# New places for the side operations of a four-layer kernel, and the order in which its waits are written

## The chip, the cores and the metric

The kernel runs on one core of one Trainium2 chip. The metric is the device time of one execution in microseconds (us); the median of several executions is given. A core has five engines that matter here, each with its own in-order stream of instructions: PE (TensorE, matrix products), DVE (VectorE), ACT (ScalarE), POOL (GpSimd) and SP, which here only issues DMAs. They meet through semaphores: an instruction that ends raises one, another instruction waits for its value.

## The reference

Thirty-two sequences of 256 rows and 256 channels pass four layers one after the other. Two of them are selective state-space layers, which are computed as a recurrence over the 256 rows; one is softmax attention with 16 heads, one is linear attention. Cut to what sets the work:

```python
def step(hst, inp):                      # layers 0 and 2, 512 channels x 16 states
    dt_t, B_t, C_t, x_t = inp
    dA = jnp.exp(dt_t[:, :, None] * A)
    hst = hst * dA + (dt_t * x_t)[:, :, None] * B_t[:, None, :]
    return (hst, jnp.einsum('bds,bs->bd', hst, C_t))

att = jnp.einsum('bnhl,bmhl->bnmh', q, k)            # layer 1
att = jax.nn.softmax(att + (1.0 - mask) * -1000000.0, axis=2)
y = jnp.einsum('bnmh,bmhl->bnhl', att, v)

attn = jnp.einsum('bhse,bhsd->bhed', softmax(k), v)  # layer 3, linear in the rows
y = jnp.einsum('bhtd,bhed->bhte', softmax(q), attn)

x = L0(x); x = L1(x); x = L2(x); x = L3(x)           # each adds its result to x
```

Every layer begins with a layer norm and is modulated by a condition vector.

## The kernel before

Two sequences form a group (512 columns side by side); there are 16 groups. The backbone of the program is the recurrence. For one layer and one group it takes 32 **steps**, each over 128 channels and two states at once (a tile of 128 x 1024). Step s consists of:

- `exp{s}` on ACT (L975): the decay factors into one of three tiles `da`;
- `dbx{s}` on DVE (L1025): the input term into the PSUM tile `z`, of which there is one;
- `scan{s}` on DVE (L1039): the recurrence along the rows, out of `da` and `z` into one of four tiles `hw`;
- `mul{s}` and `add{s}` on POOL (L1057, L1064): times C, and the two states added;
- `red{s}` on PE (L926): a product with the identity that sums in PSUM.

The four `hw` tiles are a ring: `scan{s}` waits for `red{s-4}`. `dbx{s}` waits for `scan{s-1}`, since it overwrites `z`, and `scan{s}` waits for `dbx{s}`. So DVE alternates between two operations that each wait for the one ahead of them on the same engine. SP loads the slices `bs` and `cs` of B and C for every step, broadcast to all partitions.

Everything else is a **side operation**. It is written as pieces: `front` (layer norm, input projection, convolution), `mid` and `rest` (step sizes: `d` on PE, then `ab`, `e`, `l` on ACT, `dt` on DVE, `dtx` on POOL; gates `z`), `back` (output projection, residual), `attn_a`/`attn_b` (softmax attention, one sequence each) and `lin_a`/`lin_b` (linear attention). In **one round** of the loop 64 steps are done: 32 of the first recurrence (segment 0) with the pieces attn_b, front1, rest0, back1, lin_a and mid1 beside them, and 32 of the second (segment 1) with back0, attn_a, front0, rest1, lin_b and mid0. The groups are pipelined across rounds: each segment works on other groups than the pieces beside it.

What sets the order is the table `PLACES`. For each piece and each engine it has one number for each part of that piece. A part with the number 27.73 is written on its engine behind what the recurrence puts at lower numbers: whole numbers are `dbx` on DVE, s + 0.33 is `scan` (the table `AT`), s + 0.3 is a reduction on PE, s + 0.1 an `exp` on ACT, s + 0.05 and s + 0.55 are `mul` and `add` of step s - 1 on POOL. So a DVE number between s and s + 0.33 puts an operation between `dbx` and `scan`, one between s + 0.33 and s + 1 puts it between `scan` and the next `dbx`. There is no scheduler at run time; every engine works its list off in this order and stands when the operation at its head isn't ready.

In attention, eight pairs of heads each take four score products on PE (L1277) into two of three PSUM banks; DVE takes the row maxima out of them (`mx{p}0`, `mx{p}1`, L1397), and a bank is free for a later pair when its maximum is taken. Later the products are formed again the other way round (L1304), exponentiated on ACT (L1372) and multiplied with the values (L1320).

## Time and profile before

| | |
|---|---|
| median of 3 runs | 5507.8 us (5505.3 to 5511.87) |
| the profiled execution, its own time | 5501.84 us |
| span from first to last instruction of it | 5500.1 us |
| granted TensorE clock, mean | 0.885 of full |
| busy: PE / DVE / ACT / POOL | 4551.2 / 4640.8 / 3256.8 / 4061.4 us |

The span begins with a prologue that loads weights and makes constants, then the pipeline of groups fills; from about 0.5 ms to 4.9 ms it is in its steady state, in which every round does the same work in the same order; at the end it drains. The busy share of an engine is an average over all this, so the questions of what waits for what are asked of the steady state.

### The profile page before, as it was taken

How to read it: one execution, taken by the hardware profiler on the slowest of the kernel's cores; microseconds unless marked ns; L12 is line 12 of the kernel's file. 1: busy time of each engine (PE TensorE's matmuls, PEld its weight loads, DVE VectorE, ACT ScalarE, POOL GpSimd, SP SyncE). 2: the span in 40 equal slices, each digit the busy share in tenths (PEclk: the TensorE clock that was granted, in tenths of full speed). 3: DMA queues.
4: the chain of work that ended last, by engine and by line, in shares of the span. 5: the costliest groups of instructions: out<-in, count | busy, mean ns of one | idle time of the engine just before them, and what ended most of it. 6: DMA issues, size and time to landing. Idle time of an engine off the chain costs nothing.

```text
span 5500.1 us, 54997 instructions
## 1 busy us (share of the span) xinstructions
PE 4551.2 (83%) x16792; PEld 2433.0 (44%) x16792; DVE 4640.8 (84%) x4711; ACT 3256.8 (59%) x5572; POOL 4061.4 (74%) x2838
## 2 busy tenths in 40 slices
PE   4577888988889888888888888888988888888755
PEld 1243444444444444444454444444444444444423
DVE  2729899998999899999989999999989889999373
ACT  2335566666666666666666666666666666666252
POOL 1718787887878787887878788787878778787172
PEclk8668899999999899999999999999999899998775
DMA  4616666766766666676667667676667667666161
GB/s 147 215 46 230 221 233 223 238 231 221 245 216 233 223 235 225 223 248 216 234 217 237 220 230 237 219 246 210 236 221 240 219 221 248 219 230 219 37 208 53
DMA packets 355068, 1164.54 MB, mean 212 GB/s; under 512 B 39355, under 2 KB 79348, under 8 KB 354774
## 3 DMA queue, kind: packets, MB, share of 16 engines
q1 hardware_dynamic: 310614, 1106.42, 59.6%
q10 hardware_dynamic: 44160, 54.60, 3.1%
q8 instruction: 135, 2.21, 0.2%
q14 instruction: 159, 1.30, 0.1%
HBM read 1140.78 MB, written 20.10 MB: 211 GB/s over the span
## 4 chain that ended last, share of the span: by engine, by line
PE 41%; DVE 28%; issue 10%; POOL 9%; ACT 8%; DMA 3%; SPq 1%; DVEq 0%; ACTq 0%; POOLq 0%
DVE hw L1039 15%; PE ps L926 7%; DVE ps L1025 7%; PE ps L698 5%; PE ps L1231 5%; PE ps L1277 4%; POOL hw L1057 4%; PE ps L1304 3%; PE ps L1222 3%; PE ps L1320 2%; DVE mx L1397 2%; PE ps L707 2%; ACT da L975 2%; POOL hw L1064 2%; PE ps L669 1%
## 5 line engine op out<-in xcount | busy, mean ns | idle before, releaser
L1057 POOL TENSOR_TENSOR hw<-hw,cs 128x1024 f32<-128x1024 f32 x1024 | 2413.2, 2357 | 698.7 <-DVE hw L1039 636.2
L1039 DVE TENSOR_TENSOR_SCAN hw<-da,ps 128x1024 f32<-128x1024 f32 x1024 | 2335.4, 2281 | 94.9 <-ACT da L975 21.2
L975 ACT ACTIVATE da<-dt,a_neg 128x510 f32<-128x510 f32 x2048 | 1332.1, 711 | 193.7 <-DVE hw L1039 191.2
L1064 POOL TENSOR_TENSOR hw<-hw 128x512 f32<-128x512 f32 x1024 | 1297.9, 1267 | 66.3
L926 PE MATMUL ps<-hw,ident 128*128 128x512 f32 x2048 | 1184.0, 683 | 180.7 <-POOL hw L1064 180.6
L1025 DVE TENSOR_TENSOR ps<-ps,bs 128x1024 f32<-128x1024 f32 x1024 | 1256.6, 1227 | 67.0 <-DMA bs<-bc_scratch 7.1
L926 PEld LDWEIGHTS ps<-hw,ident 128*128 128x128 f32 x2048 | 399.9, 213 | 634.0 <-issue 322.6
L698 PE MATMUL ps<-hT,w_in 128*128 128x512 f32 x1024 | 534.5, 658 | 68.7 <-DVE dt L886 47.8
L1372 ACT ACTIVATE pts<-ps 128x512 f32<-128x512 f32 x512 | 278.5, 593 | 441.7 <-PE ps L1304 441.7
L1397 DVE TENSOR_REDUCE mx<-ps 128x2 f32<-128x512 f32 x512 | 332.0, 681 | 166.5 <-PE ps L1277 165.6
L1277 PE MATMUL ps<-k,q 32*128 32x256 f32 x2048 | 354.3, 469 | 112.5 <-DVE mx L1397 112.0
L570 ACT ACT_TABLE_LOAD x319 | 409.3, 1283 | 5.6
L698 PEld LDWEIGHTS ps<-hT,w_in 128*128 128x128 f32 x1024 | 200.5, 206 | 344.8 <-issue 209.8
L1277 PEld LDWEIGHTS ps<-k,q 32*128 32x128 f32 x2048 | 217.1, 219 | 300.8 <-DVE mx L1397 183.3
L1304 PE MATMUL ps<-q,k 32*128 32x256 f32 x2048 | 301.6, 412 | 21.0 <-ACT pts L1372 21.0
L1320 PE MATMUL ps<-pts,va 128*32 128x256 f32 x2048 | 269.8, 397 | 2.8 <-ACT pts L1372 2.6
L909 POOL TENSOR_TENSOR dtx<-dt,u 128x512 f32<-128x512 f32 x128 | 162.2, 1268 | 142.8 <-DVE dt L886 142.4
L1304 PEld LDWEIGHTS ps<-q,k 32*128 32x128 f32 x2048 | 185.1, 191 | 144.7 <-ACT pts L1372 63.3
L1139 PE MATMUL ps<-w_out,dtx 128*128 128x256 f32 x1024 | 240.3, 389 | 3.4 <-DVE dtx L1008 1.8
L713 PE MATMUL ps<-xd,w_dt 97*128 97x512 f32 x256 | 170.4, 753 | 80.3 <-POOL dtx L909 54.5
L707 PE MATMUL ps<-u,taps 128*128 128x512 f32 (+3 forms) x512 | 229.0, 590 | 0.0
L1139 PEld LDWEIGHTS ps<-w_out,dtx 128*128 128x128 f32 x1024 | 195.8, 194 | 57.7 <-issue 30.8
(178 smaller groups left out, 5306.8 us busy)
## 6 DMA issues: line engine op xcount, KB each, us to landing
bs<-bc_scratch SPq DMA_DIRECT2D x1024, 512.0 KB, 4.4
cs<-bc_scratch SPq DMA_DIRECT2D x1024, 512.0 KB, 4.9
taps<-taps_scratch SPq DMA_DIRECT2D x32, 512.0 KB, 5.5
xhat<-in_x ACTq DMA_DIRECT2D x16, 512.0 KB, 7.2
gate<-gates_scratch ACTq DMA_DIRECT2D x64, 128.0 KB, 5.2
x_b<-in_x ACTq DMA_DIRECT2D x16, 512.0 KB, 7.6
x_scratch<-x_b ACTq DMA_DIRECT2D x16, 512.0 KB, 3.4
x_c<-x_scratch ACTq DMA_DIRECT2D x16, 512.0 KB, 6.4
```

What stands on the lines that cost most here:

```text
L570: nc.scalar.preload_act_table_set(name)
L698: ins = nc.tensor.matmul(side[pc.bank[f"m{m}"]], w_in[l][:, k, m * P:(m + 1) * P], hT[:, k, :], start=(k == 0), stop=(k == DC - 1))
L926: nc.tensor.matmul(yps, ident[:, :], hw[q % RING][:, 0, :], start=False, stop=(q % PER == PER - 1))\
L975: ins = nc.scalar.activation(da[q % (AHEAD + 1)][:, k, :, 1:S], dt_[:, c, :].rearrange("p (b s) -> p b s", b=GB)[:, :, 1:S], ACT.Exp, scal ...
L1025: nc.vector.tensor_tensor(z, dxp.unsqueeze(1).broadcast_to([P, 2, T]), bs[s % B_RING][:, :, :], ALU.mult)\
L1039: nc.vector.tensor_tensor_scan(tile[:, :, :].rearrange("p n t -> p (n t)"), da[s % (AHEAD + 1)][:, :, :, :].rearrange("p n b s -> p (n b s)"),
L1057: nc.gpsimd.tensor_tensor(tile[:, :, :], tile[:, :, :], cs[s % C_RING][:, :, :], ALU.mult)\
L1064: nc.gpsimd.tensor_tensor(tile[:, 0, :], tile[:, 0, :], tile[:, 1, :], ALU.add)\
L1139: ins = nc.tensor.matmul(side[pc.bank[key]][:, k * D:(k + 1) * D], dtx[l][:, c, r * P:(r + 1) * P], w_out[l][:, c, :], start=(c == 0), sto ...
L1277: ins = nc.tensor.matmul(banks[hh][:, t * S:(t + 1) * S], q4[rr, h // 4, t * P:(t + 1) * P], k4[rr, h // 4, :], start=True, stop=True)
L1304: ins = nc.tensor.matmul(banks[hh][:, t * S:(t + 1) * S], k4[rr, h // 4, t * P:(t + 1) * P], q4[rr, h // 4, :], start=True, stop=True)
L1397: nc.vector.tensor_reduce(mx[:, :, h // 4, at0], side[pc.bank[f"s{p}{hh}"]].rearrange("p (t s) -> p t s", t=RB), X, ALU.max, negate=True). ...
```

## The change

All tables in `PLACES` get new numbers: nearly every side operation on PE, ACT, DVE and POOL stands a little earlier or later among the steps. No operation is added or removed. On ACT the number of loads of function tables stays at 321. Besides, the order in which waits are written is turned in five spots: in `scan_vector` for `dbx` and for `scan`, in `times_c` for `mul`, and in `attn_tensor` for both kinds of score products.

```diff
     "mid1": {
-        "pe": [29.55, 29.675, 29.8, 29.925, 30.05, 30.175],
+        "pe": [28.586, 28.729, 28.871, 29.014, 29.157, 30.8],
...
@@ scan_vector
-                if s % PER == 0:
-                    dve.wait_ge(pc.of(f"dxp{c}"), pc.upto(g, f"dxp{c}"))
-                dve.wait_ge(*b_slice(l, g, s))
                 if s:
                     dve.wait_ge(pc.of(f"scan{s - 1}"), pc.upto(g, f"scan{s - 1}"))
...
+                if s % PER == 0:
+                    dve.wait_ge(pc.of(f"dxp{c}"), pc.upto(g, f"dxp{c}"))
+                dve.wait_ge(*b_slice(l, g, s))
                 nc.vector.tensor_tensor(z, dxp.unsqueeze(1).broadcast_to([P, 2, T]), bs[s % B_RING][:, :, :], ALU.mult)\
...
                 yield s + AT["scan"]
+                dve.wait_ge(pc.of(f"dbx{s}"), pc.upto(g, f"dbx{s}"))
                 dve.wait_ge(pc.of(f"exp{s}"), pc.upto(g, f"exp{s}"))
...
-                dve.wait_ge(pc.of(f"dbx{s}"), pc.upto(g, f"dbx{s}"))
@@ times_c
+            pool.wait_ge(pc.of(f"scan{s}"), pc.upto(g, f"scan{s}"))
             pool.wait_ge(*c_slice(l, g, s))
-            pool.wait_ge(pc.of(f"scan{s}"), pc.upto(g, f"scan{s}"))
@@ attn_tensor (both score products)
-                for hh in range(2):
+                for hh in (1, 0):
```

```order
L1025 TENSOR_TENSOR ps<-ps,bs 128x1024 [waits scan1_dve,b_slice1_1_in]
L1039 SCALAR_TENSOR_TENSOR hw<-da,ps 128x1024 [waits scan1_dve,scan1_pe,scan1_act]
L1177 TENSOR_TENSOR ps<-ps,gate 128x512 [waits front1_pool,gate0_in,front1_dve,back0_pe,front1_act,front1_pe]
L1185 TENSOR_TENSOR x_b<-x_b,ps 128x512 [waits back0_dve,residual_in]
L1177 TENSOR_TENSOR ps<-ps,gate 128x512 [waits back0_pe]
L1185 TENSOR_TENSOR x_b<-x_b,ps 128x512 [waits back0_dve]
L623 BN_STATS stats<-x_b 128x6 [waits back0_dve,back0_act,back0_pe]
```

And in the changed program:

```order
L1039 SCALAR_TENSOR_TENSOR hw<-da,ps 128x1024 [waits scan1_pe,scan1_act,scan1_dve]
L1177 TENSOR_TENSOR ps<-ps,gate 128x512 [waits front1_pool,gate0_in,front1_dve,back0_pe,front1_act,front1_pe]
L1185 TENSOR_TENSOR x_b<-x_b,ps 128x512 [waits back0_dve,residual_in]
L1177 TENSOR_TENSOR ps<-ps,gate 128x512 [waits back0_pe]
L1185 TENSOR_TENSOR x_b<-x_b,ps 128x512 [waits back0_dve]
L1025 TENSOR_TENSOR ps<-ps,bs 128x1024 [waits b_slice1_0_in,scan1_dve]
L623 BN_STATS stats<-x_b 128x6 [waits back0_dve,back0_act,back0_pe]
```

The wait of `dbx` and `scan` for DVE's own preceding operation (`scan1_dve`) has moved from the semaphore instruction onto the operation; the side operations keep their waits.

The second is DVE in segment 1, steps 11 to 13, where the maxima of `attn_a` are taken. Before:

```order
L1039 SCALAR_TENSOR_TENSOR hw<-da,ps 128x1024
L1397 TENSOR_REDUCE mx<-ps 128x2 x3
L886 SCALAR_TENSOR_TENSOR dt<-ps,dt 128x512
L1397 TENSOR_REDUCE mx<-ps 128x2
L1025 TENSOR_TENSOR ps<-ps,bs 128x1024
L1397 TENSOR_REDUCE mx<-ps 128x2 x2
L623 BN_STATS stats_b<-x_c 128x6 x2
L1397 TENSOR_REDUCE mx<-ps 128x2 x2
L628 COPY small<-one_col 128x1
L630 BN_AGGR mv_b<-stats_b 128x2 x2
L1039 SCALAR_TENSOR_TENSOR hw<-da,ps 128x1024
L1397 TENSOR_REDUCE mx<-ps 128x2 x3
```

And now:

```order
L1039 SCALAR_TENSOR_TENSOR hw<-da,ps 128x1024
L1397 TENSOR_REDUCE mx<-ps 128x2 x4
L1025 TENSOR_TENSOR ps<-ps,bs 128x1024
L1397 TENSOR_REDUCE mx<-ps 128x2 x3
L623 BN_STATS stats_b<-x_c 128x6 x2
L1397 TENSOR_REDUCE mx<-ps 128x2
L628 COPY small<-one_col 128x1
L630 BN_AGGR mv_b<-stats_b 128x2 x2
L1397 TENSOR_REDUCE mx<-ps 128x2 x5
L1039 SCALAR_TENSOR_TENSOR hw<-da,ps 128x1024
L1397 TENSOR_REDUCE mx<-ps 128x2 x2
```

Between `dbx12` and `scan12` there are nine maxima in place of four.

The third is PE at the end of segment 0, from the output product of `lin_a` (L1222, `out`) over the projection of `mid1` (L722, four products) and its step size `d0` (L713) to `rest1` (L713, L698); L926 are the reductions. Before:

```order
L926 MATMUL ps<-hw,ident 128x512
L1214 MATMUL ps<-rows,ones 128x512
L1222 MATMUL ps<-w_l_out,hT_b 128x256 x4
L926 MATMUL ps<-hw,ident 128x512
L722 MATMUL ps<-u,w_xp 96x512 x4
L713 MATMUL ps<-xd,w_dt 128x512
L926 MATMUL ps<-hw,ident 128x512 x2
L713 MATMUL ps<-xd,w_dt 128x512
L698 MATMUL ps<-hT,w_in 128x512 x4
```

And now:

```order
L926 MATMUL ps<-hw,ident 128x512
L1214 MATMUL ps<-rows,ones 128x512
L1222 MATMUL ps<-w_l_out,hT_b 128x256 x4
L926 MATMUL ps<-hw,ident 128x512
L722 MATMUL ps<-u,w_xp 96x512 x4
L713 MATMUL ps<-xd,w_dt 128x512
L926 MATMUL ps<-hw,ident 128x512 x3
L713 MATMUL ps<-xd,w_dt 128x512
L698 MATMUL ps<-hT,w_in 128x512 x2
```

The neighbours are the same, but the whole chain from `out` to `d0` stands one reduction earlier: the reduction between `out` and the projection was that of step 27 and is now that of step 26.

## Rows read from the trace of the kernel before

**Rows 1.** The page, part 1: busy us (share of span), number of instructions.
```profile
PE 4551.2 (83%) x16792; PEld 2433.0 (44%) x16792; DVE 4640.8 (84%) x4711; ACT 3256.8 (59%) x5572; POOL 4061.4 (74%) x2838
```
**Rows 2.** Windows: window, us; busy of PE, PEld, DVE, ACT, POOL; clock, DMA, GB/s.
```profile
883.48:4342.05 3458.57, 3014.19 (x11507) 1628.67 (x11506) 3169.03 (x3190) 2231.48 (x3829) 2787.95 (x1937) 0.92 0.68 229
```
**Rows 3.** Waits of DVE, 883 to 4342 us: us in total, times, longest.
```profile
DVE mx L1397 <- PE ps L1277: 77.3, 65, 3.1
DVE dt L886 <- ACT dt L823: 34.3, 24, 1.8
DVE dtx L1008 <- PE ps L926: 18.1, 29, 1.6
DVE stats L623 <- DMA xhat<-in_x: 17.5, 11, 2.3
DVE small L1564 <- ACT kT L1503: 15.3, 11, 2.6
DVE hw L1039 <- ACT da L975: 14.5, 32, 0.7
```
**Rows 4.** Timeline of DVE, bare steps, then side operations (start, us, engine, line).
```profile
2126.28 2.29 DVE L1039 TENSOR_TENSOR_SCAN hw<-da,ps 128x1024 f32<-128x1024 f32 x1
2128.67 1.23 DVE L1025 TENSOR_TENSOR ps<-ps,bs 128x1024 f32<-128x1024 f32 x1
2130.03 2.29 DVE L1039 TENSOR_TENSOR_SCAN hw<-da,ps 128x1024 f32<-128x1024 f32 x1
...
2133.79 2.29 DVE L1039 TENSOR_TENSOR_SCAN hw<-da,ps 128x1024 f32<-128x1024 f32 x1
2135.99 0.68 DVE L1177 TENSOR_TENSOR ps<-ps,gate 128x512 f32<-128x512 f32 x1
2136.77 0.69 DVE L1185 TENSOR_TENSOR x_b<-x_b,ps 128x512 f32<-128x512 f32 x1
2137.38 0.69 DVE L1177 TENSOR_TENSOR ps<-ps,gate 128x512 f32<-128x512 f32 x1
2138.10 0.69 DVE L1185 TENSOR_TENSOR x_b<-x_b,ps 128x512 f32<-128x512 f32 x1
```
**Rows 5.** Timeline of POOL in a stretch without side operations.
```profile
2110.88 1.27 POOL L1064 TENSOR_TENSOR hw<-hw 128x512 f32<-128x512 f32 x1
...
2114.53 1.27 POOL L1064 TENSOR_TENSOR hw<-hw 128x512 f32<-128x512 f32 x1
```
**Rows 6.** Timeline of PE in the scores of attn_a: two pairs of heads.
```profile
2166.74 1.31 PE L1277 MATMUL ps<-k,q 32*128 32x256 f32 x8 [1.48 <-DVE mx L1397]
2168.86 2.08 PE L1277 MATMUL ps<-k,q 32*128 32x256 f32 x8 [0.81 <-DVE mx L1397]
```
**Rows 7.** Timeline, end of segment 0, from `cv3_3` to `dt1`.
```profile
2097.12 1.02 PE L926 MATMUL ps<-hw,ident 128*128 128x512 f32 x2
2098.92 3.65 PE L722 MATMUL ps<-u,w_xp 128*96 128x512 f32 x8 [0.78 <-issue]
2106.46 0.69 DVE L886 SCALAR_TENSOR_TENSOR dt<-ps,dt 128x512 f32<-128x512 f32 x1 [1.80 <-ACT dt L823]
2112.05 0.69 DVE L886 SCALAR_TENSOR_TENSOR dt<-ps,dt 128x512 f32<-128x512 f32 x1 [1.34 <-ACT dt L823]
```
**Rows 8.** Timeline, load of the next group: `xo`, the DMA issue, first use.
```profile
2220.85 0.68 DVE L1421 TENSOR_TENSOR x_b<-ps,x_b 128x512 f32<-128x512 f32 x1
...
2221.70 0.39 ACTq L582 DMA_DIRECT2D xhat<-in_x  x1
...
2228.94 1.40 DVE L623 BATCH_NORM_STATS2 stats<-xhat 128x6 f32<-128x256 f32 x4 [1.46 <-DMA xhat<-in_x]
```
**Rows 9.** The page, part 5: the recurrence's groups with idle time before them.
```profile
L1057 POOL TENSOR_TENSOR hw<-hw,cs 128x1024 f32<-128x1024 f32 x1024 | 2413.2, 2357 | 698.7 <-DVE hw L1039 636.2
L1039 DVE TENSOR_TENSOR_SCAN hw<-da,ps 128x1024 f32<-128x1024 f32 x1024 | 2335.4, 2281 | 94.9 <-ACT da L975 21.2
L1025 DVE TENSOR_TENSOR ps<-ps,bs 128x1024 f32<-128x1024 f32 x1024 | 1256.6, 1227 | 67.0 <-DMA bs<-bc_scratch 7.1
```

More of the change, by code:

```diff
@@ L200 @@
     "mid0": {
-        "pe": [27.729, 27.871, 28.014, 28.157, 28.633, 28.967],
-        "act": [27.814, 28.5, 28.7, 28.9],
-        "dve": [31.11, 31.22],
-        "pool": [31.217, 31.383],
+        "pe": [27.9, 28, 28.1, 28.2, 28.633, 28.967],
+        "act": [28.433, 28.656, 28.767, 28.989],
+        "dve": [31.22, 31.83],
+        "pool": [31.217, 32.05],
         "sp": [30.533, 30.867],
@@ L214 @@
     "rest0": {
-        "pe": [0.633, 3.967, 4.5, 4.9, 5.967, 7.467, 8.133, 10.767],
-        "act": [-1.5, 2.3, 4.6, 4.767, 4.933, 7.8, 8.267, 8.767, 8.933],
-        "dve": [3.165, 9.165, 11.165, 13.165],
-        "pool": [3.3, 9.3, 11.3, 11.8],
+        "pe": [-1.333, 4.8, 5.7, 6.1, 6.9, 7.8, 9.78, 10.98],
+        "act": [1.767, 3.6, 5.6, 5.85, 7.7, 7.9, 8.35, 9.475, 9.6],
+        "dve": [4.165, 9.777, 10.665, 14.11],
+        "pool": [4.3, 10.3, 11.3, 15.217],
         "sp": [-0.909, -0.818],
@@ L242 @@
     "back0": {
-        "pe": [2.1, 3.467, 3.633, 3.8, 3.967],
-        "act": [1.767, 3.433, 3.767, 6.3],
-        "dve": [5.414, 5.498, 5.581, 5.665, 5.749],
-        "pool": [4.717, 4.883],
+        "pe": [3.443, 3.586, 3.729, 3.871, 4.014],
+        "act": [-1.75, 4.35, 4.85, 6.267],
+        "dve": [5.442, 5.553, 5.665, 5.777, 5.888],
+        "pool": [4.3, 4.425],
         "sp": [-0.545, -0.455],
@@ L249 @@
     "back1": {
-        "pe": [11.967, 14.05, 15.7],
-        "act": [10.6, 13.6],
-        "dve": [13.665, 14.165, 15.665, 16.11, 16.22],
-        "pool": [16.217, 16.383],
+        "pe": [11.9, 14.8, 18.767],
+        "act": [10.85, 17.35],
+        "dve": [14.22, 14.665, 16.665, 17.141, 17.189],
+        "pool": [15.383, 18.717],
         "sp": [-0.727, -0.636],
@@ L1294, in attn_tensor @@
                     banks = [side[pc.bank[f"t{p}{hh}"]] for hh in range(2)]
-                    for hh in range(2):
+                    for hh in (1, 0):
                         if p == 0 and hh == 0:
```

82 lines of the change are left out of this document (41 added, 41 removed), and 6 rows, old and new, of the table PLACES.

## The prediction, made before the changed kernel had run

> **What bounds the kernel now.** I read the page's busy times first: DVE is busy for 84% of the span, PE for 83%, POOL for 74% [rows 1]. A mean over filling and draining says little, so next the window that holds eleven whole rounds, from one start of `back0` to another: 3458.57 us, 314.4 us a round [rows 2]. There DVE is busy for 3169.03 us, 92%, PE for 87%, POOL for 81%, at a mean granted clock of 0.92. DVE is the engine that the round's length follows; what can be won is the time in which it stands, 289.5 us in the window or 26.3 us a round.
>
> That time is of two kinds. The waits list gives the long stands [rows 3]: maxima that wait for score products 77.3 us, step sizes that wait for ACT 34.3, the gated output that waits for a reduction 18.1, the statistics of the next group that wait for its DMA 17.5, the linear attention's reciprocal 15.3, scans that wait for their exponentials 14.5. These six make 177.0 us; with the smaller ones I estimate 19 us a round. The other kind no list names: in the timeline [rows 4] a scan begins at 2126.28 and lasts 2.29 us, `dbx` starts at 2128.67, 0.10 us behind it, and the next scan 0.13 us behind that one's end, though nothing but DVE's own preceding operation was awaited. The page's idle before scan and before `dbx`, 94.9 and 67.0 us in the whole run with small named parts [rows 9], is mostly this.
>
 An operation that waits for nothing fresh even starts before the one ahead has ended: the scan that began at 2133.79 ends at 2136.08, L1177 behind it starts at 2135.99, an overlap of 0.09 us. So a side operation in a gap hides the gap, and only gaps without one can win. Counted in DVE's order, before has 425 scans directly behind their `dbx` and 473 `dbx` directly behind a scan; the changed program has 468 and 547, because it bunches its side operations more. Before: 425 x 0.13 + 473 x 0.10 = 103 us. After: 1015 x 0.035 = 36 us. Against that, 117 more bare pairs lose an overlap of 0.09 us each, 10 us. Sum: -57 us. Part of it will be eaten, since DVE, arriving sooner, stands longer where PE, ACT or a DMA comes last; with a fifth off I take **-45 us**. Bounds: 0, if every time saved ends in another engine's wait, and -67 us.
>
> POOL limits this as well. Its shortest step, from one `add` to the next, is 2114.53 - 2110.88 = 3.65 us [rows 5]; DVE's bare step is now 3.75 us (2126.28 to 2130.03) and would be 3.59. Where many bare steps follow each other, POOL becomes the slower one and caps the gain at 0.10 instead of 0.16 a step. The ring of four lets DVE run ahead by some 3 steps and most bare stretches are short, so this is inside the fifth taken off. The turned waits of `mul` and of the score products I cost at nothing on the path where DVE is far ahead (POOL waits 636.2 us for scans [rows 9], it has room), and at 0.07 us for each pair of scores that DVE waits for: 0.07 x 16 pairs a round at most 1.1 us a round; I take none of it, it is in the lower bound.
>
> There is a page that speaks against this term. In the Trainium skill, VectorE: DVE Perf Modes, section "The DRAIN you can't avoid", eight copies with a semaphore after each are stated to take as long as eight with one at the end: a wait for one's own engine costs nothing. By that rule the sum would lack these 45 us. The two L1185 [rows 4] say otherwise, since the same dependence costs 0.10 or 0.03 us depending on where its wait sits.
>
> **The places, stand by stand.** Times of a stand are read per round and compared with the new order.
> - Maxima. The 77.3 us [rows 3] are 7.0 a round; by their places in the timeline 2.9 fall on `attn_b` in segment 0 and 4.1 on `attn_a` in segment 1. In `attn_b` the first moves from behind `scan4` to behind `dbx5` with `dt1` now ahead of it, 1.9 us later on DVE, the projections of keys and values that come before its products on PE stand one reduction earlier, and the input projection that stood between the first two pairs now follows the second. These stands should nearly go: -2.5.
> - In `attn_a` two pairs of products took 1.31 us near full clock and 2.08 us at half clock [rows 6]. With three banks, `mx{p}0` can't start sooner than one product time after `mx{p-1}0` ended, and between them DVE has one maximum of 0.7 us. Nine maxima now stand in one gap, with 1.1 us of statistics among them. At full clock four pairs leave about 4 x (1.3 - 0.6) - 1.1 = 1.7 us of idle, at half clock 4 x (2.2 - 0.6) - 1.1, less 1.2 us for a `dbx` within the first, = 4.1 us. PE works in bursts here, as it does now, and now it is at half clock here; I take 3.2 for the block: -0.9.
> - `dt0` of `mid1`, 1.80 us [rows 7]. The projection starts at 2098.92, behind a reduction that began at 2097.12. One reduction earlier in the list takes one of 1.02 us out from ahead of it, not a whole step, since `out` ahead of both keeps its time. 1.8 becomes 1.0: -0.8. `dt1` waits 1.34 us [rows 7] for a chain that starts at `dt0` (`dtx0`, `d1`, `ab1`, `e1`, `l1`, 5.6 us in all) over `dbx31` and `scan31`; order and chain stay, DVE gets there 0.2 us sooner: +0.2.
> - The reciprocal of the keys, 15.3 / 11 = 1.4 us [rows 3]. Its maximum moves half a step later and the chain of `front1` ahead of it on ACT gets a step more room: -1.2.
> - Scans that wait for `exp`, 1.3 us a round [rows 3], three spots. `exp2` of segment 1 now has one gate ahead of it instead of two, `exp11` of segment 0 no longer stands behind `l3`, `exp30` of segment 1 stands ahead of the convolution's end; but `exp31` then comes behind a whole `mid0` chain: -0.8.
> - The gated output, 18.1 / 11 = 1.6 us: its reductions get ahead of score products in two of three spots: -0.9.
> - The next group's load. `xo` begins at 2220.85, the DMA is issued at 2221.70 and its statistics begin at 2228.94 [rows 8], 7.4 us behind `xo`'s end. Between them now lie two scans and a `dbx` (5.9 us), then they will be two `dbx` and a scan (4.7 us): the stand grows from 1.5 to 2.7 us: +1.1.
>
> These make -2.5 - 0.9 - 0.8 + 0.2 - 1.2 - 0.8 - 0.9 + 1.1 = -5.8 us a round. A list of numbers written anew for four engines also makes stands that I haven't traced; half a microsecond at two or three spots is what before has in such small ones, so +1.3. That leaves -4.5 us a round, and 16 rounds (the last ones thin) make **-72 us**. Bounds: 0 (each stand comes back elsewhere) and -12 us a round, -190 us, if only `dt1`, the load and a few maxima are left of the 19.
>
> **Sum.** 5501.84 - 45 - 72 = 5385 us for an execution like the profiled one. The median shown is 6 us above it, 0.1%; I carry half of that over: **5388 us**, 2.2% below.
>
> **Rivals.**
> - The places bring nothing and only the waits do (each stand that goes is replaced). 5508 - 45 = 5463 us. For it: half of what the list names hangs on chains that keep their order, such as `dt1`. Against: three stands have a cause that the new order plainly removes.
> - The waits bring nothing, by the skill's rule or since POOL and PE take it back. 5508 - 72 = 5436 us.
> - The places bring more than I could trace, -10 us a round, and the waits all 57: 5508 - 217 = 5291 us.
> - Slower: TensorE takes the end. Its mean clock of 0.92 [rows 2] is a mix of full and half, so 16% of a round, 50 us, now run at half clock. A new list makes new gaps on PE, and where it stands the clock falls. Were the half-clock time doubled, 50 us of the round would do only 25 us of matmul work, at 87% busy 22 us more of PE time, against 40 us in which it stands now. A third of that, 7 us, reaching DVE would cancel the waits' and the places' gain together; half, 11 us, would give 5508 + 16 x (11 - 7.3) = 5567 us. It decides from about 35 us of additional half clock a round. Against it: score products, the one stretch where PE's stands are long, are stretches at half clock already.
> - Nothing measurable, 5508: gains cancelled by new stands.
>
> **How the numbers follow.** The forecast has a chance of 0.50 (5340 to 5440), places without effect 0.16, waits without effect 0.08, more than forecast 0.15, slower 0.07, no difference 0.04. A measurement of this kernel can tell about 0.2%, 11 us, from no change. So faster by over 0.2%: 0.89, within it 0.04, slower 0.07. The range leaves out the slower rival, no change and the far end of the best: 5300 to 5475.
>
> **What would show it.** Right: in the timeline 0.03 to 0.04 us between `dbx` and scan both ways, with the idle before L1039 and L1025 down from 162 us together to below 100, though bare pairs are more; waits of DVE for L1277 and L823 smaller, the one for the DMA of `xhat` larger, near 2.7 us a round. Wrong: gaps still at 0.10; a clock below 0.90 in the steady state; POOL's wait for scans near zero; or a DVE stand of several us in `attn_a` between `dbx12` and `scan12`.

## The result: slower, and the profile after

The changed kernel takes 5574.8 us (median of 4 runs, 5537.95 to 5590.66), the kernel before beside it 5507.4 us: ratio 1.0113, 95% interval 1.0074 to 1.0152. 5388 us had been forecast. The profiled execution, on which the rows below rest, took 5537.95 us and is the shortest of the four; what makes the others longer comes out below.

The page, part 1 (columns as in [rows 1]), and the window of eleven whole rounds (columns as in [rows 2]):

```profile
PE 4578.3 (83%) x16792; PEld 2422.8 (44%) x16792; DVE 4653.2 (84%) x4711; ACT 3259.9 (59%) x5572; POOL 4053.3 (73%) x2838
```
```profile
878.38:4373.63 3495.25, 3027.14 (x11508) 1619.32 (x11507) 3178.97 (x3190) 2234.75 (x3830) 2782.60 (x1937) 0.92 0.67 226
```

A round takes 3495.25 / 11 = 317.8 us instead of 314.4 [rows 2], at the same mean clock. DVE's work is nearly the same (3178.97 us busy for 3169.03 in the eleven rounds); what has grown is the time in which it stands.

**The short gaps are gone.** DVE's timeline of three bare steps (start, duration):

```profile
2115.97 2.29 DVE L1039 TENSOR_TENSOR_SCAN hw<-da,ps 128x1024 f32<-128x1024 f32 x1
2118.29 1.23 DVE L1025 TENSOR_TENSOR ps<-ps,bs 128x1024 f32<-128x1024 f32 x1
2119.56 2.29 DVE L1039 TENSOR_TENSOR_SCAN hw<-da,ps 128x1024 f32<-128x1024 f32 x1
```

The scan ends at 2118.26 and `dbx` starts at 2118.29; `dbx` ends at 2119.52, the next scan starts at 2119.56. In [rows 4] these gaps were 0.10 and 0.13 us. Over all bare pairs of the window the medians fall from 0.132 to 0.035 us ahead of a scan and from 0.104 to 0.035 us ahead of a `dbx`. All gaps of DVE under 0.3 us, overlaps counted as negative, sum to 32.5 us less, 3.0 us a round.

**The long stands have grown.** Those over 0.3 us rise from 208.1 to 278.5 us in the eleven rounds, by 6.4 us a round. The waits list of DVE, 880 to 4340 us (us in total, times, longest), to be held against [rows 3]:

```profile
DVE mx L1397 <- PE ps L1277: 100.2, 87, 2.5
DVE ps L1025 <- DMA bs<-bc_scratch: 46.1, 27, 3.7
DVE qsm L1557 <- PE ps L1222: 29.9, 11, 9.3
DVE dt L886 <- ACT dt L823: 22.6, 24, 1.4
DVE ps L1025 <- ACT ps L989: 17.6, 20, 2.0
DVE rec L1409 <- PE ps L1328: 17.2, 11, 1.6
```

The stands that the prediction wanted gone are smaller or not in the list: `dt` 22.6 us for 34.3, the gated output 1.1 for 18.1 and the next group's statistics 9.7 for 17.5 (both further down the list), the reciprocal of the keys gone from it. Three take their place: maxima 100.2 us for 77.3, `dbx` waiting for the B rows 46.1 us, and `qm`, the maximum over the queries of `lin_b` (L1557), 29.9 us. On the page the idle ahead of the scan falls and that ahead of `dbx` rises (to be held against [rows 9]):

```profile
L1039 DVE TENSOR_TENSOR_SCAN hw<-da,ps 128x1024 f32<-128x1024 f32 x1024 | 2333.6, 2279 | 37.0 <-ACT da L975 8.4
...
L1025 DVE TENSOR_TENSOR ps<-ps,bs 128x1024 f32<-128x1024 f32 x1024 | 1256.2, 1227 | 115.5 <-DMA bs<-bc_scratch 65.1
```

### The profile page after: what moved, and what is told of

The parts are those of the page before. It is cut to its first block, busy times and chain, and to the rows that moved or that the text cites. A ratio compares the mean times of both kernels' runs of the same rounds, so it can differ in the third digit from the quotient of the medians.

```text
span 5536.2 us, 54997 instructions
## 1 busy us (share of the span) xinstructions
PE 4578.3 (83%) x16792; PEld 2422.8 (44%) x16792; DVE 4653.2 (84%) x4711; ACT 3259.9 (59%) x5572; POOL 4053.3 (73%) x2838
## 4 chain that ended last, share of the span: by engine, by line
PE 48%; DVE 20%; ACT 10%; issue 8%; POOL 7%; DMA 5%; SPq 1%; ACTq 0%; DVEq 0%; POOLq 0%
PE ps L926 8%; DVE hw L1039 8%; PE ps L1231 5%; PE ps L1304 5%; PE ps L1277 4%; DVE ps L1025 4%; PE ps L1222 4%; POOL hw L1057 3%; PE ps L698 3%; ACT da L975 3%; PE ps L1139 3%; PE ps L707 3%; DVE mx L1397 3%; PE ps L1320 3%; DMA bs<-bc_scratch 2%
## 5 line engine op out<-in xcount | busy, mean ns | idle before, releaser
L1039 DVE TENSOR_TENSOR_SCAN hw<-da,ps 128x1024 f32<-128x1024 f32 x1024 | 2333.6, 2279 | 37.0 <-ACT da L975 8.4
L1025 DVE TENSOR_TENSOR ps<-ps,bs 128x1024 f32<-128x1024 f32 x1024 | 1256.2, 1227 | 115.5 <-DMA bs<-bc_scratch 65.1
L926 PE MATMUL ps<-hw,ident 128*128 128x512 f32 x2048 | 1178.4, 676 | 120.9 <-POOL hw L1064 120.6
L926 PEld LDWEIGHTS ps<-hw,ident 128*128 128x128 f32 x2048 | 397.4, 212 | 595.3 <-issue 326.9
L698 PE MATMUL ps<-hT,w_in 128*128 128x512 f32 x1024 | 525.3, 644 | 72.4 <-DVE dt L886 47.8
L635 POOL TENSOR_TENSOR rstd<-mv,eps 128x2 f32<-128x2 f32 (+1 forms) x96 | 18.9, 197 | 448.6 <-DVE mv L630 448.6
L1304 PE MATMUL ps<-q,k 32*128 32x256 f32 x2048 | 306.5, 419 | 33.9 <-ACT pts L1372 29.4
L698 PEld LDWEIGHTS ps<-hT,w_in 128*128 128x128 f32 x1024 | 192.0, 199 | 321.8 <-issue 181.5
L1277 PEld LDWEIGHTS ps<-k,q 32*128 32x128 f32 x2048 | 205.4, 216 | 269.1 <-DVE mx L1397 218.0
L1304 PEld LDWEIGHTS ps<-q,k 32*128 32x128 f32 x2048 | 183.3, 193 | 176.5 <-ACT pts L1372 101.3
L1207 PE MATMUL ps<-ident,xhat 128*128 128x128 f32 x256 | 52.4, 339 | 247.9 <-ACT xhat L649 247.9
```

The costliest lines, as they stand in the source:

```text
L698: ins = nc.tensor.matmul(side[pc.bank[f"m{m}"]], w_in[l][:, k, m * P:(m + 1) * P], hT[:, k, :], start=(k == 0), stop=(k == DC - 1))
L926: nc.tensor.matmul(yps, ident[:, :], hw[q % RING][:, 0, :], start=False, stop=(q % PER == PER - 1))\
L1025: nc.vector.tensor_tensor(z, dxp.unsqueeze(1).broadcast_to([P, 2, T]), bs[s % B_RING][:, :, :], ALU.mult)\
L1039: nc.vector.tensor_tensor_scan(tile[:, :, :].rearrange("p n t -> p (n t)"), da[s % (AHEAD + 1)][:, :, :, :].rearrange("p n b s -> p (n b s)"),
L1277: ins = nc.tensor.matmul(banks[hh][:, t * S:(t + 1) * S], q4[rr, h // 4, t * P:(t + 1) * P], k4[rr, h // 4, :], start=True, stop=True)
L1304: ins = nc.tensor.matmul(banks[hh][:, t * S:(t + 1) * S], k4[rr, h // 4, t * P:(t + 1) * P], q4[rr, h // 4, :], start=True, stop=True)
```

## The experiments

Seventeen more kernels ran. Each is given with its ratio to the kernel before on the same chip; 0.2% is 11 us. The ratio compares means and each chip has its own before (5495 to 5507 us in the median), so a difference of two medians from different chips can be off by some 10 us, and where it matters both are given. The last three columns are worked out from the profile of each over ten steady rounds: length of a round, sum of DVE's stands over 0.3 us in it, and TensorE's time at half clock (1.2 GHz) in it.

| kernel | median us | ratio (95%) | round | stands | half clock |
|---|---|---|---|---|---|
| before | 5507.4 | 1 | 314.7 | 19.2 | 49.5 |
| the change | 5574.8 | 1.0113 (1.0074 to 1.0152) | 318.2 | 25.7 | 50.2 |
| e1_waits | 5450.8 | 0.9908 (0.9893 to 0.9923) | 312.3 | 21.3 | 46.1 |
| e2_places | 5618.9 | 1.0222 (1.0195 to 1.0248) | 323.3 | 26.1 | 62.2 |
| e3_load | 5587.9 | 1.0156 (1.0134 to 1.0178) | 321.1 | 28.8 | 59.3 |
| e4_qm | 5569.7 | 1.0124 (1.0106 to 1.0141) | 321.5 | 29.2 | 60.1 |
| e5_seg0 | 5449.7 | 0.9913 (0.9900 to 0.9927) | 311.3 | 19.2 | 41.3 |
| e6_seg1 | 5564.6 | 1.0125 (1.0103 to 1.0146) | 320.2 | 29.0 | 63.5 |
| e7_attnvec | 5492.3 | 0.9991 (0.9980 to 1.0003) | 314.7 | 23.7 | 45.7 |
| e8_early | 5445.2 | 0.9907 (0.9892 to 0.9921) | 311.3 | 20.2 | 43.0 |
| e9_red | 5544.6 | 1.0071 (1.0054 to 1.0088) | 318.5 | 25.9 | 52.9 |
| e10_s7 | 5485.4 | 0.9969 (0.9957 to 0.9981) | 313.7 | 21.3 | 52.2 |
| e11_vecold | 5580.8 | 1.0148 (1.0133 to 1.0162) | 319.2 | 26.4 | 52.6 |
| e12_scan13 | 5444.5 | 0.9907 (0.9891 to 0.9924) | 312.6 | 20.2 | 44.7 |
| e13_petoo | 5599.6 | 1.0191 (1.0171 to 1.0211) | 321.2 | 29.8 | 57.3 |
| e14_k_after | 5492.9 | 0.9991 (0.9978 to 1.0003) | 314.6 | 21.9 | 45.3 |
| e15_k_seg1 | 5474.2 | 0.9958 (0.9944 to 0.9971) | 311.7 | 20.4 | 43.7 |
| e16_k_load | 5502.6 | 1.0006 (0.9995 to 1.0018) | 314.8 | 22.7 | 43.9 |
| e17_k_load_red | 5501.4 | 1.0004 (0.9992 to 1.0015) | 314.9 | 22.8 | 44.2 |

### The two parts apart

`e1_waits` has the new order of waits and the old table of places, `e2_places` the new table and the old order.

> Places of before, waits in the order of the change. Theory W (the turned waits work, the new places lose): the short gaps between dbx and scan fall from 0.13 and 0.10 to 0.035 us; that is 264 x 0.097 + 297 x 0.069 = 46 us in eleven rounds, 4.2 us a round, and with a fifth eaten by stands some 3.3 us a round: 5507 - 53 = 5455 us. Rival (what DVE saves, the loads of bs take back, since a bare step is then 3.6 us and a load takes 4.5 to 8 us): stands on bs appear as in the changed kernel, 1 us a round or more, and the time stays above 5485 us.

> Places of the change, waits in the order of before. Theory W: all of the loss comes from the places, and the waits' gain is missing: the changed kernel's median 5575 us + 352 x 0.069 + 264 x 0.097 (some 4.5 us a round, a fifth of it not felt) = about 5630 us, ratio to before 1.022. Rival (the shorter step makes the loss, places and waits don't go together): between 5500 and 5560 us, with the stands on bs gone.

Both came as expected. The waits give 0.9% on the old places (1 to 0.9908, 51 us) and 1.1% on the new (1.0222 to 1.0113; 60 us, 44 by the medians); the places cost 2.2% with the old waits and 2.05% with the new, 113 to 122 us. The parts add up: the waits are a gain of some 50 us, and the loss is the places'. The five turned waits, three of them on POOL and PE, were never run apart. DVE's short gaps alone shrink by 4.8 us a round in e1_waits and its stands over 0.3 us grow by 2.3 (over eleven rounds), so no other part is needed for the 2.4 us by which the round is shorter; that the others give nothing isn't shown. The groups of the recurrence in e1_waits, from the page:

```profile
L1039 DVE TENSOR_TENSOR_SCAN hw<-da,ps 128x1024 f32<-128x1024 f32 x1024 | 2334.9, 2280 | 66.3 <-PE ps L926 23.1
...
L1025 DVE TENSOR_TENSOR ps<-ps,bs 128x1024 f32<-128x1024 f32 x1024 | 1256.8, 1227 | 37.1 <-ACT ps L989 10.6
```

Idle of 103.4 us together, where [rows 9] had 161.9, with every side operation in its old place.

### Two stands taken away, and paid back

The largest new stands of the change were `dbx0` of segment 1 (2.9 us a round) and `qm` (2.8). The first is a matter of DMA. `back0` now issues its gates and 512 KB of residual on ACT's queue just ahead of the first B rows of segment 1 (first the loads, then the DMA of the B rows on SP's queue, then the `dbx` that waits for it):

```profile
2105.39 0.81 ACTq L586 DMA_DIRECT2D gate<-gates_scratch  x2
2106.24 0.45 ACTq L592 DMA_DIRECT2D x_b<-in_x  x1
...
2106.57 1.61 SPq L1097 DMA_DIRECT2D bs<-bc_scratch  x2
...
2114.70 1.23 DVE L1025 TENSOR_TENSOR ps<-ps,bs 128x1024 f32<-128x1024 f32 x1 [2.49 <-DMA bs<-bc_scratch]
```

Two delays add up here. The store of the B and C rows, which the first slice waits for, is issued 2.6 us ahead of these loads and lands after 4.1 us instead of 2.2 (medians of ten rounds, the store ahead of segment 1); the first slice itself lands after 8.0 us instead of 5.7. The first delay isn't made by the loads, as the traces of two kernels further down show: `e5_seg0`, in which they are late, has it (3.9 us), `e8_early`, in which they are early, doesn't (2.2). It comes with the new lists beside scan0. The second comes with the loads: the slice took 6.7 us in e8_early and 5.5 in e3_load. With only one of the two, `dbx0` stands 0.4 us or less. The store in a round of the change, of e5_seg0 and of e8_early (size, us to landing):

```profile
bc_scratch<-xd SPq DMA_DIRECT2D x1, 64.0 KB, 3.7
```
```profile
bc_scratch<-xd SPq DMA_DIRECT2D x1, 64.0 KB, 4.2
```
```profile
bc_scratch<-xd SPq DMA_DIRECT2D x1, 64.0 KB, 2.1
```

`e3_load` puts these loads behind the start of scan1, `e4_qm` puts `qm` and its subtraction a step later:

```
back0, act:   [-1.75, 4.35, ...] -> [2.3, 4.35, ...]                     e3_load
lin_b, dve:   [..., 15.165, 15.665, 16.165, ...] -> [..., 15.165, 16.553, 17.12, ...]   e4_qm
```

> The changed kernel with one number of back0 on ACT back from -1.75 to 2.3, so that the loads of the gates and of the residual for back0 are issued behind the second exponential of segment 1 and not at its start. Theory: the 512 KB of x_b stand in the way of the small store of the B and C rows (1.7 us in before, 3.7 us now) and of the first slice bs; without them the store is back under 2.5 us, DVE's stand at the first dbx of segment 1 (2.9 us a round) falls below 0.7 us, and the time falls by up to 2.5 x 16 = 40 us against the changed kernel, to 5535 us. Rival (the store waits for its rows, xd, which come later now): the stand stays above 2 us and so does the time.

> The changed kernel with the maximum and the difference of q in lin_b (L1557, L1560) one step later on DVE. Theory: DVE stands 2.7 us a round at L1557 only because it comes there before PE has got to the product; one step later (4 us) the stand is gone, PE's list is what it was, and 2 to 2.5 us a round are won: 5575 - 35 = 5540 us. Rival (PE's list of products in that stretch is the path, and DVE only waits for it elsewhere): the stand at L1409 (1.6 us a round) or at the scans grows by what L1557 loses, and the time stays at 5575 us.

Both missed. In e3_load the stand at `dbx0` fell from 2.9 to 0.3 us a round and `qm` rose to 5.2; in e4_qm the one at `qm` went and `dbx16`, one operation further on, stood 3.8 us. The waits lists of e3_load and e4_qm:

```profile
DVE mx L1397 <- PE ps L1277: 116.1, 92, 3.0
DVE qsm L1557 <- PE ps L1222: 47.3, 11, 9.3
```
```profile
DVE ps L1025 <- ACT ps L989: 45.8, 27, 5.9
```

Whatever DVE does first behind the maxima waits. The late one is TensorE's and ScalarE's chain, not one operation of DVE. (The 5.2 us at `qm` in e3_load aren't all repayment: four of its rounds have the long stand of 9.3 us that is looked at below, where the profile of the change has one. The same edit without such rounds, e16_k_load, settles it.)

### Which half

Side operations belong to a segment. `e5_seg0` has the new lists of attn_b, front1, rest0, back1, lin_a and mid1 (beside scan0) and of mid0, and the old ones of the rest; `e6_seg1` the new ones beside scan1 (mid0 is new in both).

> Half of the places. The new order of waits everywhere; the lists attn_b, front1, rest0, back1, lin_a and mid1 (all that is placed beside scan0) and mid0 are the new ones, the lists beside scan1 (back0, attn_a, front0, rest1, lin_b) are the old ones. Theory A (the loss lies beside scan1: in the traces of before and of the change VectorE's stands beside scan0 fall from some 8.3 to 6.0 us a round, those beside scan1 rise from 10.7 to 18.2): about 2 us a round less than with all old places and the new waits (5450.8), so 5415, between 5400 and 5440. Theory B (the loss comes from the density of the new places as a whole, by more half clock and more traffic on the DMA queues at once): half of the 124 us, about 5510.

> The other half. The new order of waits; the lists beside scan0 (attn_b, front1, rest0, back1, lin_a, mid1) are the old ones, back0, attn_a, front0, rest1, lin_b and mid0 the new ones. Theory A: the whole loss and more, since what the lists beside scan0 gave is gone too: 5450.8 + 8 to 10 us a round over some 15 rounds, 5590, between 5565 and 5620. Theory B: about 5510.

Theory A held, in its main point: e5_seg0 stands at e1_waits (0.9913 against 0.9908), e6_seg1 at 1.0125. The new lists beside scan0 neither give nor cost anything in time (35 us of gain had been expected), and the whole loss lies beside scan1. The waits of e5_seg0, then of e6_seg1:

```profile
DVE mx L1397 <- PE ps L1277: 54.0, 64, 2.6
```
```profile
DVE mx L1397 <- PE ps L1277: 124.6, 86, 2.9
DVE qsm L1557 <- PE ps L1222: 73.2, 11, 9.3
```

### Parts of that half

`e7_attnvec` has one new list on the old places, VectorE's of attn_a (nine maxima in one gap). `e8_early` has one other, ScalarE's of back0 (the early loads). `e11_vecold` is the mirror of e7: the change with the old list of VectorE for attn_a. `e13_petoo` is e7 with TensorE's new list of attn_a as well.

> One list alone: all old places and the new waits, but VectorE's list of attn_a is the new one (nine maxima in the stretch behind scan 11 where there were three, the rest behind dbx 12; the sum of rows and the new rows of x two steps earlier). TensorE's and ScalarE's lists stay. If the dense block of maxima costs by itself (their products take 2.1 us each at half clock), the stands of the block rise by some 3 us a round and the time from 5450.8 to about 5500. Rival: the stands come from TensorE's and ScalarE's lists around it, and VectorE's list alone costs under 1 us a round: 5440 to 5467.

> One list alone: all old places and the new waits, but ScalarE's list of back0 is the new one (the loads of the gates and of 512 KB of residual go out at -1.75 and not at 1.767, ahead of scan1's first steps; the rest of the list hardly moves). If the loads beside the stores and loads of the B and C rows delay dbx0 for good, the time rises by the 2.6 us a round that dbx0 stands longer in the change: about 5490. Rival, after the run in which the change had these loads back at 2.3 and gained nothing: the delay is made up again behind dbx0, where VectorE waits for others, and the time stays within 0.2% of 5450.8.

> The mirror of e7_attnvec: the changed kernel, but VectorE's list of attn_a is the old one (three maxima where the change has nine; qa, the sum of rows and the new rows of x later). If that list costs the 41 us that it cost on the old places whatever stands around it, the time is 5574.8 - 41 = 5534, between 5515 and 5550. Rival: the new lists of TensorE and ScalarE were fitted to the new list of VectorE, so that the old one makes them wait as well: 5560 or more.

> e7_attnvec with TensorE's list of attn_a new as well (red9 between the score products of pairs 4 and 5, red10 between 6 and 7, each t and pv product where the change has it); all other lists are the old ones, the waits the new. Theory: the 114 us between e1_waits (5450.8) and e6_seg1 (5564.6) are those two lists of attn_a: 41 by VectorE's (e7_attnvec, 5492.3) and most of the other 72 by TensorE's, so 5540 to 5565. Rival: the lists of VectorE and TensorE were fitted to each other, and the other 72 us come with lin_b, rest1, front0 and ScalarE's lists: 5475 to 5510.

The list of maxima costs 41 us on the old places, 0.8%. Taken out of the new ones it gains nothing: DVE then stands 3.0 us at `mx00` and 3.4 at `qm`. The early loads cost nothing at all: their stand of 2.9 us exists only together with the new lists beside scan0 (in e6_seg1, which has the early loads and all other new lists beside scan1, `dbx0` stands 0.1 us, and its loss is that of the change). And e13_petoo costs more than all of e6_seg1, and more than either of its forecasts (5565 at most), since it makes a stand of its own: 4.5 us a round at `dt2`, whose product on TensorE now comes behind projections of attn_a that the old list of rest1 doesn't allow for. Lists fitted to each other can't be priced by swapping one of them; e13_petoo and e11_vecold say little on the change itself. What was left was to look at what sets the 9.3 us.

### What makes 9.3 us at `qm`

In the profile of the change, `qm` stands 1.8 to 2.6 us in nine of ten steady rounds and 9.3 us in one; in e6_seg1 9.3 us in six of ten. There the six rounds take 323.4 us in the mean, the other four 315.3. Two rounds of the change, the long one and the next. First the long one: TensorE's products from the first transposed score (L1304) to the query product, then DVE, then the window (columns as in [rows 2]; the clock is the last but two):

```profile
2190.74 1.13 PE L1304 MATMUL ps<-q,k 32*128 32x256 f32 x8
2193.04 1.68 PE L1304 MATMUL ps<-q,k 32*128 32x256 f32 x8 [1.17 <-ACT pts L1372]
...
2198.52 2.07 PE L1304 MATMUL ps<-q,k 32*128 32x256 f32 x8
...
2206.97 3.75 PE L1222 MATMUL ps<-w_l_q,hT_b 128*128 128x256 f32 x8
```
```profile
2210.76 0.69 DVE L1557 TENSOR_REDUCE qsm<-ps 128x32 f32<-128x512 f32 x1 [9.30 <-PE ps L1222]
```
```profile
2193.00:2210.00 17.00, 16.96 (x58) 8.22 (x59) 8.38 (x8) 10.11 (x18) 10.52 (x6) 0.51 0.47 162
```

And the next round:

```profile
2515.35 1.13 PE L1304 MATMUL ps<-q,k 32*128 32x256 f32 x8
2517.65 1.13 PE L1304 MATMUL ps<-q,k 32*128 32x256 f32 x8 [1.17 <-ACT pts L1372]
...
2525.84 1.99 PE L1222 MATMUL ps<-w_l_q,hT_b 128*128 128x256 f32 x8
```
```profile
2527.87 0.69 DVE L1557 TENSOR_REDUCE qsm<-ps 128x32 f32<-128x512 f32 x1 [1.82 <-PE ps L1222]
```
```profile
2510.00:2527.00 17.00, 15.43 (x93) 9.18 (x92) 15.30 (x14) 10.29 (x20) 11.76 (x7) 0.97 0.53 175
```

It is the same work in the same order. From the second transposed score to the end of the query product it takes 2210.72 - 2193.04 = 17.7 us at a granted clock of 0.51 and 2527.83 - 2517.65 = 10.2 us at 0.97; the difference, 7.5 us, is that between the two stands. In the long round the clock falls at 2193.49, 0.45 us into the products behind the 1.17 us in which TensorE waits for the exponentials of the first score, and comes back at 2210.56. In the other it is the same stand, and the clock holds. The two rounds aren't alike ahead of it: in the long one TensorE had been at half clock for 17.1 us from step 10 on (2166.18 to 2169.60 and 2173.01 to 2186.66), in the other for 10.2 (2500.69 to 2510.93). But other rounds of the change with 17.1 and 20.5 us there kept the clock. What decides isn't shown; the fall is a risk that goes with this stand. The kernel before has the key product of lin_b in that stand; the change has moved it ahead of both. `e14_k_after` puts it back in the change, `e15_k_seg1` in e6_seg1:

```
lin_b, pe:   [12.5, 13.1, 15.157, ...] -> [12.5, 13.9, 15.157, ...]
```

> The changed kernel with one of TensorE's places of lin_b moved: the key product of the linear attention (1.9 us, L1231) goes from ahead of the first transposed score product of attn_a to between the first and the second (13.1 becomes 13.9), as in the kernel before. In the change TensorE stands 1.17 us between the two, until ScalarE has the exponentials of the first; in the round in which VectorE stands 9.3 us at qm its granted clock is full up to this stand and half from it on. Theory: with the product in the stand TensorE keeps its clock, the stands of 9.3 us at qm are gone in every round, and the median, in which I estimate some five rounds have one more of them than the profiled run had, falls from 5574.8 by 30 to 40 us to about 5540. Rival: the clock falls at qm anyway, since other stands remain, or the later key product makes its own stand at kb0: 5565 to 5590.

> The same single place in e6_seg1, where 6 of the 10 rounds looked at stood 9.3 us at qm instead of 1.8 to 2.6. Theory: none does, which is 6 x 7.5 / 10 = 4.5 us a round; less 0.5 us for a stand at kb0 over 15 rounds, 5564.6 - 60 = 5505, between 5485 and 5530; half clock at steps 14 and 15 falls from 10.0 us a round to near 0. Rival: 5550 or more.

One number in a table of 466 gives 82 us in the change and 90 us in e6_seg1 by the medians, 67 and 92 us by the ratios, more than expected. TensorE in e14_k_after, same place:

```profile
2186.72 1.13 PE L1304 MATMUL ps<-q,k 32*128 32x256 f32 x8
2187.78 1.99 PE L1231 MATMUL ps<-hT_b,w_l_k 128*128 128x256 f32 x8
2189.70 1.13 PE L1304 MATMUL ps<-q,k 32*128 32x256 f32 x8
...
2197.60 1.99 PE L1222 MATMUL ps<-w_l_q,hT_b 128*128 128x256 f32 x8
```

The key product fills the stand, no round is long any more, and half clock at steps 14 and 15 falls from 10.0 to 0.0 us a round in e15. All nineteen profiles, with 14 rounds each that have this chain in segment 1, say the same. Seven have the key product ahead of the first score (the change, e2, e3, e4, e6, e9, e11), and 1, 5, 4, 5, 9, 2 and 2 of their rounds are at half clock through the chain; in the other twelve, where it stands between the first two scores, no round is. The waits lists of e14_k_after, then e15_k_seg1:

```profile
DVE qsm L1557 <- PE ps L1222: 7.8, 11, 1.4
```
```profile
DVE qsm L1557 <- PE ps L1222: 9.4, 11, 1.4
```

Two things are in this. `qm` also stands 1.2 us less in the rounds that were short already, since what precedes the scores no longer waits for the key product: over 15 rounds some 18 us. The other 49 us (64 by the medians) would be, by 7.5 us each, six or seven long rounds (eight or nine) in the mean run of the change. The profiled run had one and is 37 us shorter than the median, five times 7.5, which gives six. The three runs without a profile show a mean clock of 0.874 to 0.878 where the profiled one has 0.886, which is 100 to 145 us more at half clock, or six to nine times the 17 us of a long round. These are estimates that agree roughly; only the profiled runs show their rounds. Between the two profiled runs themselves, 5537.95 and 5493.07 us, `qm` makes 27 of the 45 us, and the rest is spread over other stands.

### What is left

`e9_red` puts the scores of pairs 5 and 6 ahead of `red9` in the change; `e10_s7` those of pair 7 ahead of `red10`, `e12_scan13` scan13 ahead of the last maxima, both in e5_seg0; `e16_k_load` and `e17_k_load_red` repeat e3 and e9 with the key product in its place.

```
attn_a, pe:   [..., 11.1, 11.8, 12.05, 12.7, ...] -> [..., 11.1, 11.12, 11.14, 12.7, ...]      e9_red
attn_a, pe:   [..., 11.167, 12.5, ...] -> [..., 11.167, 11.6, ...]                             e10_s7
attn_a, dve:  [..., 13.082, 13.165, 13.248, 13.665, ...] -> [..., 13.553, 13.665, 13.777, 14.165, ...]  e12_scan13
```

> The changed kernel with two of TensorE's places of attn_a moved: the score products of pairs 5 and 6 (11.8 and 12.05 become 11.12 and 11.14) stand ahead of red9 again, as in the kernel before; red9 and red10 follow them. In the change red9, which takes 2.08 us at half clock, stands between the products of pairs 4 and 5 and VectorE stands 2.5 us at the maximum of pair 5; with the old order that stand was 0.9. Theory: the stand falls by 1.6 us a round, the time from 5574.8 by 1.6 x 15 to about 5550. Rival, after the two runs in which a stand was taken away and came back behind it: TensorE's chain behind the block ends when it did, the stand comes back at qm or dbx16, and the time stays within 0.3% of 5574.8.

> e5_seg0 with one of TensorE's places moved: the score products of pair 7 in attn_a (12.5 becomes 11.6) go ahead of red10. In e5_seg0 VectorE stands 2.0 us a round at the maximum mx70, since TensorE runs red10 (2.08 us at half clock) first, which only scan14 needs. Theory: the stand goes, and with it 2 us x 15 = 30 us: 5420. Rival: as in e3_load and e4_qm, the time is made up of TensorE's and ScalarE's chain behind the block, and the stand comes back at qa0, dbx16 or yg1: 5440 to 5455.

> e5_seg0 with four of VectorE's places of attn_a moved: scan13 goes ahead of mx70, mx71 and qa0 (13.082, 13.165, 13.248 become 13.553, 13.665, 13.777) and dbx14 ahead of qa1 (13.665 becomes 14.165). TensorE's list stays. The scan (2.29 us) lies in the 2.0 us in which VectorE stands at mx70 while TensorE does red10, so the maxima come some 0.3 us later than before and the rest of the chain with them. Theory: 1.7 to 2.0 us a round less, 5449.7 - 27 = 5423. Rival, as in e10_s7: another timing of the block costs TensorE its full clock elsewhere in the round and the time is 5445 or more.

> e14_k_after with the loads of back0 at 2.3 instead of -1.75, the edit of e3_load. There it took 2.6 us a round out of the stand at dbx0 and the time rose, while VectorE stood longer at qm, with TensorE at half clock. Theory: with the key product in its place that repayment is gone and the load's price shows: 2.6 us a round over 15 rounds less some new small stands, 5492.9 - 30 = 5463, between 5445 and 5475. Rival: VectorE, arriving sooner, stands longer in the block of maxima and at the gates whatever the clock does: 5480 to 5500, as e8_early had no price either.

> e16_k_load with the score products of pairs 5 and 6 of attn_a ahead of red9 too, the edit of e9_red. There the stand at mx50 fell by 1.2 us and that at mx70 grew by 1.2. Theory: the same here, the time within 0.2% of e16_k_load. Rival: 15 to 25 us less, as the medians of the change and of e9_red (5574.8 and 5544.6) would have it.

In e9_red the stand at `mx50` fell by 1.2 us and that at `mx70` rose by 1.2. Its median is 30 us lower (23 by the ratio) and meets the 5550 us that had been expected, but not for the reason given: the stands of the block are 7.5 us a round in both. Its interval touches the change's, and e17 against e16 shows no difference: no price. e10_s7 shortened the stand at `mx70` by 1.2 us, got 2.3 us at `qa0` in its place, and lost full clock at steps 20 and 21 (0.0 to 6.4 us a round): 36 us slower than e5_seg0. e12_scan13 filled its stand and stood 2.6 us at `dbx16` for 0.4: no gain. Their lists, e10_s7, then e12_scan13:

```profile
DVE q L1404 <- PE ps L1287: 32.8, 20, 2.4
```
```profile
DVE ps L1025 <- ACT ps L989: 43.6, 22, 3.0
```

e16_k_load took the stand at `dbx0` from 2.7 to 0.4 us again, and again got it back elsewhere: `dbx8` 1.8 for 0.4, `mx00` 2.1 for 1.0, `dbx4` 0.8. So the clock was not what took that gain back; ScalarE's dxp and the products are due when they are.

The maxima of attn_a stand 6.9 us a round in e14_k_after and 7.6 in e15_k_seg1, 3.3 in e1_waits. These 3.6 and 4.2 us are 54 and 64 us in 15 rounds; e14 is 0.8% and e15 0.5%, 46 and 27 us, above e1_waits. So the block is large enough to be the remainder, in e15 more than twice over. It was priced once, on the old places (41 us, e7_attnvec), and not by undoing it beside the mended key product: what makes the remainder isn't shown.

No version beat the new waits on the old places. e1_waits, e5_seg0, e8_early and e12_scan13 lie within 0.1% of each other, at 0.991 of the kernel before.

## Why the prediction was wrong

**The bound** was read rightly: DVE sets the round, and each time change followed its stands.

**The waits** were right. Forecast -45 us with bounds 0 and -67; measured 51 us on the old table and 44 to 60 on the new.
**The places: the step that failed**, -72 us forecast, +113 to +122 measured. Stand by stand, us a round in the profiles:

| term | forecast | measured |
|---|---|---|
| maxima of attn_b | -2.5 | -1.5 |
| maxima of attn_a | -0.9 | +3.5 |
| `dt0`, `dt1` | -0.6 | -1.0 |
| reciprocal of the keys | -1.2 | -1.4 |
| scans waiting for `exp` (measured: for reductions too) | -0.8 | -1.8 |
| gated output | -0.9 | -1.5 |
| load of the next group | +1.1 | -0.8 |
| stands not traced | +1.3 | +11.0 |

The stands that the prediction named as going did go, nearly to size, but for the maxima of attn_a; the one that it had growing, the next group's load, shrank. These are lengths of stands and not prices. Three steps were wrong, by weight:
1. "So +1.3" for the stands that had not been traced. They were 11.0: `dbx0` 2.9, `qm` 2.8, `dbx14` and `dbx16` of segment 0 2.3, the rest under 1 each. Of these only what stands behind `qm` proved to have a price: the key product's place, 67 to 82 us of the 113 to 122. The value was taken from small stands of the kernel before, and nothing in the new order was read for it. The key product's move, one row on PE, is visible in the order; the prediction looked at DVE's order and, of PE's, at the end of segment 0.
2. The block of attn_a, "3.2 for the block". The row of 2.08 us [rows 6] was there, but the sum allowed only for products between the maxima. In the new order `red9` and `red10` stand among them. PE in the change, then DVE:

```profile
2173.80 2.08 PE L1277 MATMUL ps<-k,q 32*128 32x256 f32 x8 [1.19 <-DVE mx L1397]
2175.80 2.08 PE L926 MATMUL ps<-hw,ident 128*128 128x512 f32 x2
2177.80 2.08 PE L1277 MATMUL ps<-k,q 32*128 32x256 f32 x8
2180.66 2.07 PE L1277 MATMUL ps<-k,q 32*128 32x256 f32 x8 [0.78 <-DVE mx L1397]
2182.67 2.08 PE L926 MATMUL ps<-hw,ident 128*128 128x512 f32 x2
```
```profile
2179.91 1.29 DVE L1397 TENSOR_REDUCE mx<-ps 128x2 f32<-128x512 f32 x2 [2.53 <-PE ps L1277]
2182.77 1.29 DVE L1397 TENSOR_REDUCE mx<-ps 128x2 f32<-128x512 f32 x2 [1.56 <-PE ps L1277]
```

The reduction `red9`, which begins at 2175.80, stands between two scores, and the maximum behind them waits 2.53 us. That the reduction stands there isn't what the block costs, since e9_red took it away and the block stood 7.5 us a round as before. The prediction's last paragraph had named such a stand as what would show it wrong.

3. Half clock was weighed as a sum, in the slower rival at 0.07: "it decides from about 35 us of additional half clock a round". The profiled round has 50.2 us of it, before 49.5, and still is longer; in the three longer runs the mean clock, 0.874 to 0.878 for 0.885 before, gives some 6 to 9 us a round more, far from 35. It decides by where it lies: in a long round 17 us of it under the chain of scores, exponentials and values cost 7.5 us of that round. Half clock elsewhere shows no such price (e5_seg0 has 6.8 us a round at steps 18 and 19 of scan0, where before has none, and is as fast as e1_waits), but e5_seg0 has also lost some 10 us of it at other steps of scan0, so that isn't a clean comparison. This rival's time, 5567 us, lies next to the measured 5574.8 by luck: its doubled half clock did not come. The fall behind short stands agrees with the Trainium skill (TensorE: Matmul & The Clock Gate, section "A second HAM failure mode: psum-queue depth-cycling"), which tells of a kernel whose TensorE idles briefly between groups of products and swings between its two clocks; here the stand was 1.17 us, and filling it was worth 67 to 82 us.

A last error was one of form: each stand was subtracted as if it were time. The stands taken away in e3_load, e4_qm, e9_red, e10_s7, e12_scan13 and e16_k_load came back behind, where the next result of the same chain was due. What made the round shorter was an edit to the late chain itself.

## What to carry to other kernels

A stand is worth its length only if what is late after it isn't on the same chain; find the engine whose chain is late behind the stand, and shorten or fill that one.
